# Mean-free output weights, a bias by matrix product, fewer K copies and a 16-column router in a transformer layer on one core

## The reference

```python
x = x + LN(attn(LN(x)) @ Wo + b_out)      # 32 query heads and 8 K/V heads of size 8, RoPE, causal softmax
x = x + LN(ffn(LN(x)))                    # router of 8 experts, top 2, plus 2 shared experts, inner size 640
# RoPE: concat([x1*c - x2*s, x2*c + x1*s])
# router: scores = sigmoid(x @ w_router.T); the two best, their weights divided by their sum
```

## Time and profile before

| | us |
|---|---|
| median of 3 runs | 797.37 (796.3 to 798.7) |
| profiled execution, its own time | 796.7 |
| its span | 794.9 |
| TensorE busy | 710.2 |
| VectorE busy | 617.5 |
| ScalarE busy | 449.7 |
| GpSimd busy | 323.8 |

### The profile page before, as it was taken

The page is one execution under the profiler, slowest core; times in us unless marked ns, Lnnn a source line. Parts: engine busy times, 40 slices in busy tenths (PEclk is TensorE's granted clock), DMA queues, the critical chain, the costliest instruction groups (busy, mean ns, idle before and its releaser), DMA issues. The chain is left out here.

```text
span 794.9 us, 15235 instructions
## 1 busy us (share of the span) xinstructions
PE 710.2 (89%) x5746; PEld 576.0 (72%) x5746; DVE 617.5 (78%) x1364; ACT 449.7 (57%) x745; POOL 323.8 (41%) x450
## 2 busy tenths in 40 slices
PE   4667888888888898998999899999999999999994
PEld 2334445555555555576888899999999999988884
DVE  5997888888888778655586688888888888847885
ACT  3546565666666665733424477777777777732231
POOL 4323334444443343710022444445444453127854
PEclk9999999999999999999999999999999999999998
DMA  7000000000000000000012466676766777513221
GB/s 265 1 1 4 3 2 10 9 9 10 9 9 9 10 12 12 16 9 13 1 59 91 158 236 224 228 237 209 238 213 228 240 204 237 186 35 89 89 68 53
DMA packets 29128, 74.28 MB, mean 93 GB/s; under 512 B 4608, under 2 KB 18304, under 8 KB 29056
## 3 DMA queue, kind: packets, MB, share of 16 engines
q0 software_dynamic: 12208, 55.45, 21.4%
q1 hardware_dynamic: 16432, 17.20, 6.5%
q10 hardware_dynamic: 416, 0.66, 0.3%
HBM read 62.68 MB, written 10.22 MB: 92 GB/s over the span
## 5 line engine op out<-in xcount | busy, mean ns | idle before, releaser
L955 DVE TENSOR_TENSOR HF<-SS,PS 128x256 f32<-128x256 f32 (+1 forms) x155 | 75.9, 490 | 97.3 <-ACT SS L705 56.7
L793 DVE TENSOR_REDUCE NM<-PS 128x2 f32<-128x512 f32 (+1 forms) x192 | 124.4, 680 | 13.8 <-PE PS L395 13.8
L705 ACT ACTIVATE SS<-PS 128x256 f32<-128x256 f32 (+1 forms) x155 | 68.0, 439 | 116.6 <-PE PS L395 111.4
L395 PE MATMUL PS<-XGH,WH 128*128 128x256 f32 x460 | 129.9, 282 | 2.8 <-DVE WL L1053 2.8
L395 PE MATMUL PS<-XGL,WH 128*128 128x256 f32 x460 | 129.5, 281 | 0.0
L395 PE MATMUL PS<-XGH,WL 128*128 128x256 f32 x460 | 129.4, 281 | 0.0
L1149 POOL TENSOR_SCALAR_AFFINE_SELECT PF<-PF 128x512 f32<-128x512 f32 x128 | 82.8, 671 | 97.7 <-ACT PF L667 97.7
L1053 DVE TENSOR_TENSOR WL<-RAW,WH 128x768 fp32r<-128x768 f32 x125 | 120.0, 962 | 3.3 <-ACT WH L630 3.3
L395 PE MATMUL PS<-WH,HH 128*128 128x256 f32 x390 | 112.1, 288 | 0.9 <-DVE ACC L966 0.9
L630 ACT ACTIVATE HH<-HF 128x256 fp32r<-128x256 f32 (+1 forms) x155 | 72.1, 465 | 71.1 <-DVE HF L955 66.8
L395 PE MATMUL PS<-WL,HH 128*128 128x256 f32 x390 | 110.2, 282 | 0.0
(11 more groups left out here) (169 smaller groups left out, 1475.8 us busy)
## 6 DMA issues: line engine op xcount, KB each, us to landing
ys<-YO SPq DMA_DIRECT2D x23, 256.0 KB
RAW<-in_wsh SPq DMA_DIRECT2D x4, 768.0 KB, 6.5
X<-in_x SPq DMA_DIRECT2D x8, 256.0 KB, 6.2
xn<-YY SPq DMA_DIRECT2D x16, 128.0 KB, 1.7
out<-X SPq DMA_DIRECT2D x16, 128.0 KB
QT<-NMT SPq DMA_DIRECT2D x96, 4.0 KB
RAW<-in_wsh SPq DMA_DIRECT2D x2, 384.0 KB, 6.8
XG<-xn,XIDX POOLq DMA_INDIRECT x46
```

Source lines behind the costliest of these rows:

```text
L395: return eng.matmul(o, l, r, start=start, stop=stop, skip_group_check=True)
L705: t = eng.activation(SS[:, i % 2, 0:n], bank(b, 0, n), ACT.Silu)
L793: eng.tensor_reduce(o, i, AXX, ALU.max, negate=True).then_inc(free[c], 1)
L955: eng.tensor_tensor(HF[:, c % 2, 0:n], SS[:, c % 2, 0:n], bank(b, 512 - n, 512) if n == 256 else bank(b), ALU.mult).then_inc(free[b], 1)
```

## The change

The mean over the columns is taken off Wo's rows and off the bias once, on chip (`prepare`), so that the output product has mean zero and the norm behind it needs only the division. The bias is split into three bfloat16 parts, brought to three partitions by DMA, and added by one product of three rows. `b_out`'s result is copied by ScalarE; `b_norm` is gone, and `b_add` is one fused multiply-add. The later back stages move ahead by three quarter steps. K's parts are laid out so that one copy writes three parts in both halves. RoPE's two half products become one with the halves read in swapped order. The router's weights lie as [high, rest], so that four products of 16 columns replace eight of 8; `pick` gets one more step that adds the halves, and ScalarE's exponential becomes its step 1.

```diff
-BACK = [("b_turn", 47), ("b_out", 51), ("b_stats", 51), ("b_dev", 51), ("b_norm", 56), ("b_add", 59),
-        ("b_stats2", 59), ("b_dev2", 59), ("b_norm2", 66), ("b_turn2", 71), ("b_route", 75)]
+BACK = [("b_turn", 47), ("b_out", 51), ("b_stats", 51), ("b_dev", 51), ("b_add", 56),
+        ("b_stats2", 56), ("b_dev2", 56), ("b_norm2", 63), ("b_turn2", 68), ("b_route", 72)]
-PICK = {4: [(0, k) for k in range(4)], 5: [(0, 4), (0, 5)], 6: [(0, 6), (0, 7)], 7: [(0, 8)],
-        8: [(1, k) for k in range(9)]}
+PICK = {4: [(0, k) for k in range(5)], 5: [(0, 5), (0, 6)], 6: [(0, 7), (0, 8)], 7: [(0, 9)],
+        8: [(1, k) for k in range(10)]}
...
-        if n == 0:
-            out.append(("router_split", 0))
+        if 1 <= n < 8:
+            out.append(("prepare", n - 1))
...
                 elif what == "b_out":
                     read(e, ("b_turn", i))
-                    e.wait_ge(d_wo, 16)
+                    e.wait_ge(wo_c, 2)
+                    e.wait_ge(d_b3, 48)
                     c = take(s)
+                    mm(bank(c, 0, 256), ones3[:, :], B3[:, :], True, False)
                     for k in range(2):
-                        t = mm(bank(c, 0, 256), CTT[:, i % 2, 128 * k:128 * k + 128], WO[:, k, :], k == 0, k == 1)
+                        t = mm(bank(c, 0, 256), CTT[:, i % 2, 128 * k:128 * k + 128], WO[:, k, :], False, k == 1)
...
-                        for a, r in ((XH, WRH), (XH, WRL), (XL, WRH), (XL, WRL)):
-                            t = mm(bank(c, 0, 8), a[:, k, 128 * i:128 * i + 128], r[:, 8 * k:8 * k + 8], n == 0, n == 7)
-                            n += 1
+                        for a in (XH, XL):
+                            t = mm(bank(c, 0, 16), a[:, k, 128 * i:128 * i + 128], WRX[:, k, :, :].rearrange("p a e -> p (a e)"),
+                                   k == 0 and a is XH, k == 1 and a is XL)
...
+                elif what == "b_out":
+                    made(e, s)
+                    made(e, ("b_turn2", i - 2))
+                    e.wait_ge(d_xn[i % 2], 16 * (i // 2))
+                    copy(YY[:, i % 2, :], bank(c, 0, 256)).then_inc(free[c], 1)
...
-                eng.tensor_tensor(rb[:, :, 0:4], qk[:, :, 4:8], S[:, :, 0:4], ALU.mult)
-                eng.tensor_tensor(rb[:, :, 4:8], qk[:, :, 0:4], S[:, :, 4:8], ALU.mult).then_inc(r_a, 1)
+                eng.tensor_tensor(rb, qk[:, :, ::-1, :], S, ALU.mult).then_inc(r_a, 1)
...
-                eng.tensor_copy(K[:, :, 0:4:3, :], R[:, 32:40, :].unsqueeze(2).broadcast_to([P, 8, 2, 8]))
-                eng.tensor_copy(K[:, :, 5, :], R[:, 32:40, :]).then_inc(k_1, 1)
+                eng.tensor_copy(K[:, :, :, 1:6:2, :], R[:, 32:40, :].unsqueeze(2).unsqueeze(3).broadcast_to([P, 8, 2, 3, 8])).then_inc(k_1, 1)
...
-                eng.tensor_copy(K[:, :, 1:5:3, :], Rt[:, 32:40, :].unsqueeze(2).broadcast_to([P, 8, 2, 8])).then_inc(k_3, 1)
+                eng.tensor_copy(K[:, :, :, 2:5:2, :], Rt[:, 32:40, :].unsqueeze(2).unsqueeze(3).broadcast_to([P, 8, 2, 2, 8])).then_inc(k_3, 1)
...
-                eng.tensor_tensor(K[:, :, 2, :], Rt[:, 32:40, :], K[:, :, 1, :], ALU.subtract).then_inc(k_4, 1)
-                e.wait_ge(k_4, i + 1)
-                eng.tensor_copy(KC[:, T, :, 1, :], KC[:, T, :, 0, :]).then_inc(k_5, 1)
+                eng.tensor_tensor(K[:, :, :, 0, :], Rt[:, 32:40, :].unsqueeze(2).broadcast_to([P, 8, 2, 8]), K[:, :, :, 2, :],
+                                  ALU.subtract).then_inc(k_4, 1)
...
+            def prepare(k):
+
+                if k < 3:
+                    e.wait_ge(d_bo if k == 2 else d_wo, 16)
+                    src = BO if k == 2 else WO[:, k, :]
+                    eng.bn_stats(BN[:, 48 + k, :], src[:, :]).then_inc(wo_s, 1)
+                    e.wait_ge(wo_s, 2 * k + 1)
+                    eng.bn_aggr(MV[:, 48 + k, :], BN[:, 48 + k, :]).then_inc(wo_s, 1)
+                    e.wait_ge(wo_s, 2 * k + 2)
+                    eng.tensor_scalar(src[:, :], src[:, :], MV[:, 48 + k, 0:1], None, ALU.subtract, ALU.bypass).then_inc(wo_c, 1)
+                elif k == 3:
+                    e.wait_ge(wo_c, 3)
+                    eng.tensor_copy(BB[:, 0, :], BO[0:1, :]).then_inc(wo_c, 1)
+                    e.wait_ge(wo_c, 4)
+                    eng.tensor_tensor(BR[:, 0, :], BO[0:1, :], BB[:, 0, :], ALU.subtract).then_inc(wo_c, 1)
+                elif k == 4:
+                    e.wait_ge(wo_c, 5)
+                    eng.tensor_copy(BB[:, 1, :], BR[:, 0, :]).then_inc(wo_c, 1)
+                    e.wait_ge(wo_c, 6)
+                    eng.tensor_tensor(BB[:, 2, :], BR[:, 0, :], BB[:, 1, :], ALU.subtract).then_inc(wo_c, 1)
+                elif k == 5:
+                    w = WRF[:, :].rearrange("p (k e) -> p k e", e=8)
+                    e.wait_ge(d_wr, 16)
+                    eng.tensor_copy(WRX[:, :, 0, :], w).then_inc(wrs, 1)
+                    e.wait_ge(wrs, 1)
+                    eng.tensor_tensor(WRX[:, :, 1, :], w, WRX[:, :, 0, :].bitcast(F32), ALU.subtract).then_inc(wrs, 1)
...
+                if k == 0:
+                    for t in range(t0, t0 + n):
+                        read(e, ("b_route", t))
+                    t = eng.tensor_tensor(ES[:, t0:t0 + n, :], EW[:, t0:t0 + n, 0:8], EW[:, t0:t0 + n, 8:16], ALU.add)
...
-                    eng.tensor_tensor(YY[:, i % 2, :], bank(c, 0, 256), BO[:, :], ALU.add).then_inc(free[c], 1)
...
-                elif what == "b_norm":
-                    e.wait_ge(b_rs, i + 1)
-                    normed(YY[:, i % 2, :], YY[:, i % 2, :], 16 + i).then_inc(b_yn, 1)
-                elif what == "b_add":
-                    e.wait_ge(b_yn, i + 1)
-                    eng.tensor_tensor(X1[:, i, :], X1[:, i, :], YY[:, i % 2, :], ALU.add).then_inc(b_x1, 1)
+                elif what == "b_add":
+                    e.wait_ge(b_rs, i + 1)
+                    eng.scalar_tensor_tensor(out=X1[:, i, :], in0=YY[:, i % 2, :], scalar=RS[:, 16 + i:17 + i], in1=X1[:, i, :],
+                                             op0=ALU.mult, op1=ALU.add).then_inc(b_x1, 1)
...
+                elif what == "prepare" and i == 4:
+                    e.wait_ge(wo_c, 7)
+                    for r in range(3):
+                        eng.dma_start(B3[r:r + 1, :], BB[:, r, :]).then_inc(d_b3, 16)
```

More of the change, by code:

```diff
@@ L236, in build @@
         CR = sb("CR", [P, 256], BF16)
+        EW = sb("EW", [P, NT, 2 * NE], F32)
         ES = sb("ES", [P, NT, NE], F32)
@@ L244, in build @@
         WRF = sb("WRF", [P, 16], F32)
-        WRH = sb("WRH", [P, 16], F32R)
-        WRL = sb("WRL", [P, 16], F32R)
+        WRX = sb("WRX", [P, 2, 2, 8], F32R)
+        BB = sb("BB", [1, 3, 256], BF16)
+        BR = sb("BR", [1, 2, 256], F32)
+        B3 = sb("B3", [3, 256], BF16)
+        ones3 = sb("ones3", [3, 128], BF16)
         att = ExitStack()
@@ L337, in build @@
         zero, zpad = sem("zero"), sem("zpad")
+        wo_s, wo_c, d_b3 = sem("wo_s"), sem("wo_c"), sem("d_b3")
         f_st, f_mv, f_ve, f_rs, f_xn = (sem(n) for n in ("f_st", "f_mv", "f_ve", "f_rs", "f_xn"))
-        b_st, b_mv, b_ve, b_rs, b_yn, b_x1 = (sem(n) for n in ("b_st", "b_mv", "b_ve", "b_rs", "b_yn", "b_x1"))
+        b_st, b_mv, b_ve, b_rs, b_x1 = (sem(n) for n in ("b_st", "b_mv", "b_ve", "b_rs", "b_x1"))
         c_st, c_mv, c_ve, c_rs, c_x2, c_xh = (sem(n) for n in ("c_st", "c_mv", "c_ve", "c_rs", "c_x2", "c_xh"))
@@ L343, in build @@
         q_1, q_2, q_3, q_4 = (sem(f"q_{k}") for k in range(1, 5))
-        k_1, k_2, k_3, k_4, k_5 = (sem(f"k_{k}") for k in range(1, 6))
+        k_1, k_2, k_3, k_4 = (sem(f"k_{k}") for k in range(1, 5))
         v_1 = sem("v_1")
@@ L523, in ranks @@
             def ranks():
-                e.wait_ge(picked[0], 9)
-                e.wait_ge(picked[1], 9)
+                e.wait_ge(picked[0], 10)
+                e.wait_ge(picked[1], 10)
                 e.wait_ge(d_cr, 16)
@@ L568, in _ @@
                 elif what == "k":
-                    spread(s, k_5, lambda n: KC[:, i % 2, n, :, :].rearrange("p u d -> p (u d)"))
+                    spread(s, k_4,lambda n: KC[:, i % 2, n, :, :].rearrange("p u d -> p (u d)"))
                 elif what == "pass1":
@@ L682, in _ @@
                     made(e, s)
-                    copy(ES[:, i, :], bank(c, 0, 8)).then_inc(free[c], 1)
+                    copy(EW[:, i, :], bank(c, 0, 16)).then_inc(free[c], 1)
                 elif what == "split":
@@ L723, in _ @@
                     copy(YO[:, q % 2, :, :].rearrange("p q d -> p (q d)"), bank(b)).then_inc(free[b], 1)
-                elif what == "pick" and s[2] == 0:
+                elif what == "pick" and s[2] == 1:
                     t0, n = PICKS[i]
-                    for t in range(t0, t0 + n):
-                        read(e, ("b_route", t))
+                    e.wait_ge(picked[i], 1)
                     es = ES[:, t0:t0 + n, :].rearrange("p t e -> p (t e)")
@@ L1009, in _ @@
                     divide(i)
-                elif what == "b_out":
```

(17 more changed lines are left out.)

35 lines of the change are left out of this document (17 added, 18 removed).

## The result

| | us | ratio to the kernel before, 95% interval |
|---|---|---|
| kernel before, beside it | 797.51 (796.3 to 798.7, 4 runs) | |
| changed kernel, first measurement | 807.43 (805.65 to 808.31, 4 runs) | 1.0122 [1.0098, 1.0146] |
| the same kernel in four later measurements | 800.17, 799.10, 799.51, 800.19 (34 runs, 797.09 to 802.34) | 1.0024, 1.0019, 1.0017, 1.0019; the first [1.0011, 1.0037] |

The account below looks back on a forecast made before the run. Bound: TensorE's queue waiting for three PSUM banks that go round, not VectorE's work. Start +1.3, attention +0.1 +2.6 +0.3 +2.1, hand-over -2.6 -0.45 +0.2 -0.8: +2.8 on 797.4 gives 800.2 us, range 790 to 806.

Parts of the forecast that it names:

- Whatever is won or lost ahead of it is carried to the end one for one: Changes before the routed block stage's start at 438 us reach the kernel's end in full; nothing behind it is edited.
- the dear case: Rival: `prepare` at 4.5 us, lock, bias product and clock all cost: 807 us; 804 and up counted, 18%.
- step 8: Hand-over to the dense stage: `b_norm2` earlier shortens TensorE's stall; -2.6, -0.45, +0.2, and -0.8 for the clock.
- Step 1: Bias product in `b_out`, each full period: between nothing and 0.28 us, taken as 0.13.
- Step 2 to 4: Full attention periods: XL waits for XH behind the exponential, delaying `turn` and `back`; +0.37 us each, +2.6 for seven.
- the ring: In attention, TensorE's in-order queue waiting for three PSUM banks that go round closes each period, not VectorE's sum.
- Step 5: Two periods without Q transposes, from 284 us: `back` waits for the router copy's bank; +1.1 each, +2.1 together.
- Step 6: Bias add, a norm and a second add leave VectorE: no change in the steady state.
- VectorE is the pace: Rival: VectorE sets the period, some 1.3 us a tile won over seven full periods: 786 us, 12%.
- Step 7: The start: VectorE savings -1.0 over five tiles, `prepare`'s extra work +2.3; together +1.3 us.
- The lock: Moved `b_norm2` may wait for the port pair shared with GpSimd's masking: 0.28 us a period; nothing in the sum.

Follow-up runs that it names:

- order_old: Changed kernel with the later back stages at their old places, all other edits kept: 796.06 us, ratio 0.9967.
- moved_only: Kernel before with only the back stages behind `b_norm` moved ahead by three quarter steps: 797.74 us, ratio 1.0000.
- after_again: Changed kernel, unedited, measured once more: 800.17 us.
- turn2_67: Changed kernel with `b_turn2` one quarter step earlier, ahead of `pass2`, so XH is copied ahead of the exponential: 788.44 us, ratio 0.9881.
- before_67: Kernel before with only back stages moved: three quarter steps earlier, and `b_turn2` four, ahead of `pass2`: 787.26 us, ratio 0.9863.
- after_c: Changed kernel, unedited, measured again in another call: 799.51 us.
- after_b: Changed kernel, unedited, measured a third time in another call: 799.10 us.
- more_load: Changed kernel with SyncE loading the second shared expert's weights six times more beside the last stage's gathers: 799.68 us, ratio 1.0028.
- direct: Changed kernel with GpSimd's 32 indirect gathers of expert results replaced by plain SyncE transfers, rows not picked: 798.68 us, ratio 1.0003.
- fill_pe: Changed kernel with 96 more wait instructions at the start of TensorE's program: 805.5 us, ratio 1.0084.
- fill_pe16: Changed kernel with 16 more wait instructions at the start of TensorE's program: 799.58 us, ratio 1.0025.
- hybrid: Changed kernel with back stages at old places for the first six sequences, moved earlier only for the last four tiles: 792.21 us, ratio 0.9920.

## Why the prediction was right and wrong

TensorE's waits over 0.1 us in one full period go with the period's length in every variant. They are read as the brackets of its timeline are, from one `turn` to the next:

| kernel | `turn` or XL | router copy | `back`, QT | other | sum | period |
|---|---|---|---|---|---|---|
| before | 0.54 | | 1.45 | 0.93 | 2.92 | 19.85 |
| order_old | 0.51 | | 1.45 | 1.15 | 3.11 | 19.96 |
| moved_only | 1.41 | | 0.51 | 1.09 | 3.01 | 20.09 |
| changed (after_again) | 1.41 | 0.47 | 0.51 | 1.09 | 3.48 | 20.31 |
| turn2_67 | 0.51 | 0.47 | 0.51 | 0.93 | 2.42 | 19.15 (next 19.30) |
| before_67 | 0.58 | | 0.51 | 0.93 | 2.02 | 19.02 (next 18.92) |

The period less the sum is 16.7 to 17.1 us in all six: TensorE's own work, which the edits hardly change.

**Step that failed.** "Whatever is won or lost ahead of it is carried to the end one for one." At 701 us the sum of +2.8 stood at +2.9; the last stage then added 8.4 us that no edit put there: 94.55 us in place of 86.18, most of it in a stretch in which TensorE started its products late. Why it did stays open. The argument for the step looked only at what the change touches and at what the block stage waits for; it gave no chance to a disturbance of an untouched stage, and the range ended at 806 for the dear case alone. In the later measurements the step holds (last stage 86.25 to 87.10 in their four profiles, against 86.18), and the kernel lies 1.7 to 2.3 us above the one before, where the forecast was +2.8.

**Luck in the +2.9.** Two misses cancel in it. Up to the dense stage's first product the changed kernel loses 7.2 us where steps 1 to 7 sum to 6.4, and the hand-over gives back 4.5 where step 8 has 3.65. The seven full periods up to 255 us alone cost 3.5 in place of 2.6.

**Step 1, the bias product** (+0.13 a period): order_old, which has the product and no move, is 0.11 longer. That fits, but order_old has the other edits too; the product alone was not tried.

**Step 2 to 4, the ring** (20.2 us): 20.31. XL waits 0.95 us for XH in each period, as foretold, the first maximum stands behind it, and so does `turn`:

```profile
212.44 0.38 ACT L636 ACTIVATE XH<-PS 128x256 fp32r<-128x256 f32 x1
```

```profile
212.85 0.42 DVE L1071 TENSOR_TENSOR XL<-PS,XH 128x256 fp32r<-128x256 f32 x1 [0.95 <-ACT XH L636]
213.19 0.68 DVE L800 TENSOR_REDUCE NM<-PS 128x2 f32<-128x512 f32 x1
```

It is moved_only, which has the wait and no other edit, and turn2_67, which has every edit but the wait, that show what the move costs. Not foreseen was the wait of 0.47 us for the bank of the router's 16 columns; its copy stands behind the exponential, ahead of QT. I had it only for the periods without Q transposes.

**Step 5** (+2.1 for the two): right, taken where the step took it, at `pass2`. The two periods last from 284.10 to 315.21 us before and from 288.26 to 321.68 in the changed kernel, 31.11 against 33.42, +2.3. From `turn` to `turn` they grow by only 0.7 (16.2 and 14.4 against 15.1 and 14.8), for the last `turn` comes 1 us behind its `pass2` in both kernels (0.97 and 1.07), where the one before it comes 3.78 us behind in place of 2.48.

**Step 6, VectorE's savings are worth nothing**: right, shown three times (order_old against before, turn2_67 against before_67, moved_only against changed). Only their size was off: busy time fell by 9.8 us (617.5 to 607.7), not by 20. A full period has 1.0 us less (16.39 against 17.39), and `prepare`'s three groups add 0.95 each, the sum of the three rows shown below; the rest of the difference is not accounted for. The rival "VectorE is the pace" is refuted at periods down to 19.0 us.

**Step 7, the start** (+1.3): right as far as a profile can tell. At the fifth `turn` (112.54 against 111.31) the changed kernel is 1.2 us behind. The distances between the first three `turn`s of the changed kernel are 15.1 and 18.1 us, against 15.7 and 16.5 before and 15.8 and 16.5 in moved_only, which has no `prepare`. So the savings give 0.6 back in the first (-1.0 was forecast over five tiles), and `prepare` takes 1.6 in the second, net of the savings (+2.3 was forecast for all of it). In after_again the first distance is 14.3, but that is the clock: it was granted at 0.99 there and at 0.89 in the 15.1 and the 15.7 us. In before_67 the second distance is 18.7 without `prepare`, at a granted clock of 0.82. VectorE's timeline of after_again has the first group of `prepare` between two maxima, without idle time, where the kernel before had 0.59 us of it:

```profile
59.73 0.42 DVE L839 BATCH_NORM_STATS2 BN<-WO 128x6 f32<-128x256 f32 x1
60.18 0.18 DVE L841 BATCH_NORM_AGGREGATE MV<-BN 128x2 f32<-128x6 f32 x1
60.40 0.35 DVE L843 TENSOR_SCALAR WO<-WO,MV 128x256 f32<-128x256 f32 x1
60.67 1.28 DVE L800 TENSOR_REDUCE NM<-PS 128x2 f32<-128x512 f32 x2
```

The first `turn` itself falls between 42.0 us (after_c, granted clock 1.00 up to there) and 44.2 us (after_again, 0.89) in profiles of one and the same program, so that two profiles have to be compared at the same clock.

**Step 8, the hand-over** (-3.65 in all): 98.18 us in place of 102.67, -4.5. The stall is 1.75 us where 1.7 was forecast, and the clock over the 40 us from 360 is 1.00, so the clock gave back the whole 1.6 us of which I had counted half. That is the size that was off. Half was no bad guess all the same: after_b, the same program, has a low clock at another place of the stage, from 348 to 354 us, and loses 1.5 us there.

**The lock** (0.28 us in the dear case). In the kernel before it is VectorE that is held up, at its cast of the low K part, which takes 0.65 us beside a masking of GpSimd (220.70 to 222.11):

```profile
221.54 0.65 DVE L775 CAST KC<-RT 128x128 bf16<-128x128 f32 x1
```

In the same place of a period of the changed kernel, VectorE's moved `b_norm2` and, below it, GpSimd's maskings:

```profile
223.85 0.40 DVE L746 TENSOR_SCALAR YY<-X,MV,RS 128x256 f32<-128x256 f32 x1
```

```profile
217.39 1.22 POOL L1177 TENSOR_SCALAR_AFFINE_SELECT PF<-PF 128x512 f32<-128x512 f32 x2 [3.55 <-ACT PF L673]
...
223.39 2.43 POOL L1177 TENSOR_SCALAR_AFFINE_SELECT PF<-PF 128x512 f32<-128x512 f32 x2 [3.94 <-ACT PF L673]
```

The norm and the two casts and two subtractions behind it (224.17 to 225.33) take their usual times, and the two maskings beside them take 2.43 us in place of 1.22: the first 0.63, the second up to 225.82. Here GpSimd waits, and no row shows a wait for it. The term of nothing was right. The Trainium skill (SBUF — State Buffer, section "Who interferes with whom") says that whoever issues first gets the shared pair of ports. The rows agree as far as they go: the first masking, issued ahead of the norm (223.39 against 223.85), is not held up, and the second, which starts behind it, is. That the norm starts 0.17 us before the first masking ends fits no strict lock, but GpSimd's spans in a profile are rough.

**What stays open.** What made the gap of 8.4 us: it came with one measurement and not with the program. The runs exclude the program, with its places and its gathers, as the only cause, and more_load this core's DMA load up to 0.9. Whether it was the chip, the loading of that one measurement, or something beside it is open: the later ones ran on two chips, and on which the first ran is not known. The Trainium skill (NOTIFIC — the notification-queue block, section "Overflow: three behaviours, one of which stalls the engine") says that the path on which engines write their records can hold an engine up when it fills; no run here shows whether it did.

## What to carry to other kernels

Where one queue of products goes round a few banks, look for the small copy that stands behind a long one on the evicting engine: placing the back stages so that one 0.38 us copy stands ahead of a 1.34 us exponential won 1.3 to 1.4% (before_67 against moved_only and against the unedited kernel), while 1.24 us of work a tile taken off the busiest-looking engine won nothing. Sum the waits of the pacing engine over one period and compare kernels by that sum; where the engine's own work stays the same, as here, it gives the period to within about 0.2 us and names who makes the difference. And where a difference arises in a stage that was not edited, measure the same kernel once more, separately, before explaining it: four experiments here were built to remove a gap that was not in the repetition either. Compare the granted clock of each stage before comparing its length.

## What was not expected of the hardware

- A TensorE that starts one product each 1.41 us, with its operands there and no wait shown, from 731.57 to 735.80 us in the profile of one measurement and in none of the four later profiles. The granted clock is at its lower level behind it, 0.83 over those 20 us.
- The block stage, the same in all these kernels, has three lengths, and the granted clock tells them apart. It takes 257.3 us in direct, fill_pe, fill_pe16 and moved_only, where the clock is 1.00 all through, and 258.7 to 258.8 in all others but hybrid, which have one stretch of 3.4 us at the lower level (1.2 GHz) at its head. hybrid has two such lengths in one, 6.8 us (0.83 over the 20 us from 430), and takes 259.9. TensorE's wait ahead of the stage's first product is 2.82 us with the low stretch and without. One such stretch costs 1.1 to 1.5 us, as much as the effects looked for here; others stand at 22, 42 or 370 us in some profiles and are missing in others, also of one program. The ten microseconds in question, in after_again and in moved_only:

```profile
440.00:450.00 10.00, 7.43 (x50) 7.46 (x51) 5.32 (x10) 3.10 (x7) 4.67 (x4) 0.83 0.57 192
```

```profile
440.00:450.00 10.00, 7.96 (x66) 7.78 (x66) 6.84 (x15) 3.79 (x8) 5.44 (x6) 1.00 0.45 157
```

- Instructions that only wait for something long there are not free: with 16 of them TensorE's first product starts at 7.46 us, with 96 at 14.90, so at least 93 ns each.
